# Column sums by adding tiles of every third column, and row moves by transfers, in a two-image attention and DCT kernel

## The reference

```python
yi = jnp.einsum('blc,bqc->blq', wn, xp)              # keys l, queries q
yi = jax.nn.softmax(yi * SOFTMAX_SCALE, axis=1)      # over the keys
yi = yi.reshape(B, L, H, W)
yt = jax.vmap(tconv)(yi, raw_w)                      # 6 x 6 kernel, stride 2
yd = lax.conv_general_dilated(yt, Wd, (2, 2), ((1, 1), (1, 1)), ...)
x = x + (yd + bd) / 6.0
x = x + dct2(groupnorm(x))
```

## Time and profile before

| what | us |
|---|---|
| time, median of 3 runs | 286.29 (285.88 to 287.45) |
| the profiled execution | 286.1 |
| span of its trace | 284.3 |
| PE busy | 216.6 |
| DVE busy | 154.6 |
| ACT busy | 137.5 |
| POOL busy | 94.5 |

### The profile page before, as it was taken

One profiled execution on the slowest core, in us unless ns is written; L12 is line 12 of the kernel. 1 busy time (PEld: TensorE's weight loads), 2 busy tenths in 40 slices (PEclk: granted clock), 3 DMA queues, 4 the chain that ended last, 5 costly groups with the idle time before them and its releaser, 6 DMA issues.

```text
span 284.3 us, 4211 instructions
## 1 busy us (share of the span) xinstructions
PE 216.6 (76%) x1522; PEld 200.9 (71%) x1522; DVE 154.6 (54%) x303; ACT 137.5 (48%) x273; POOL 94.5 (33%) x96
## 2 busy tenths in 40 slices
PE   0064755653647998699998999999898999995085
PEld 0033735553537997699998999999787999994083
DVE  1863134477444367567656554577878544535812
ACT  1366053955866655575776553766454331221030
POOL 8300106063522973149306161596184000000000
PEclk9999999955755999799999999999999999999555
DMA  7206985000200009910000000004000000000502
GB/s 184 35 5 89 101 117 141 1 2 0 42 15 0 3 0 100 113 18 2 2 0 2 0 2 0 2 0 85 1 1 2 0 2 0 2 0 0 109 18 42
DMA packets 9059, 8.82 MB, mean 31 GB/s; under 512 B 7696, under 2 KB 7696, under 8 KB 8560
## 3 DMA queue, kind: packets, MB, share of 16 engines
q1 hardware_dynamic: 9040, 8.56, 18.8%
HBM read 3.32 MB, written 1.18 MB: 16 GB/s over the span
## 4 chain that ended last, share of the span: by engine, by line
PE 48%; DVE 20%; ACT 12%; issue 9%; SPq 5%; DMA 3%; POOL 2%; DVEq 0%; ACTq 0%; POOLq 0%
PE zt L629 22%; PE yt L644 8%; PE ps L609 6%; DVE negm L1010 4%; DVE bnst L893 4%; PE pm L676 3%; DVE yl L1025 3%; ACT nt L807 2%; SPq L363 2%; ACT zneg L749 2%; PE pd L656 2%; ACT z L751 2%; DVE v L1048 2%; DMA v<-mimg 2%; SPq L359 2%
## 5 line engine op out<-in xcount | busy, mean ns | idle before, releaser
L629 PE MATMUL zt<-ident,nt 128*125 128x128 f32 (+1 forms) x720 | 90.6, 277 | 0.0
L629 PEld LDWEIGHTS zt<-ident,nt 128*125 128x125 f32 (+1 forms) x720 | 87.4, 179 | 0.8
L478 POOL TENSOR_TENSOR nt<-nt 128x599 f32<-128x599 f32 (+1 forms) x42 | 56.9, 1354 | 32.2 <-ACT nt L815 25.0
L1025 DVE TENSOR_TENSOR yl<-zt,yh 125x384 fp32r<-125x384 f32 (+1 forms) x60 | 33.4, 557 | 46.2 <-ACT yh L823 18.2
L823 ACT ACTIVATE yh<-zt 125x384 fp32r<-125x384 f32 (+1 forms) x60 | 29.2, 486 | 36.9 <-PE zt L629 36.9
L807 ACT ACTIVATE nt<-ps,negm 128x576 f32<-128x576 f32 x32 | 23.8, 742 | 44.6 <-DVE negm L1010 44.6
L468 POOL TENSOR_TENSOR ml<-vim,mh 128x384 fp32r<-128x384 f32 x12 | 12.3, 1029 | 61.9 <-ACT mh L783 61.8
L815 ACT ACTIVATE nt<-nt,rps 128x599 f32<-128x599 f32 x36 | 28.7, 797 | 5.0 <-DVE rps L1017 4.8
L1048 DVE SCALAR_TENSOR_TENSOR v<-pd,v 32x384 f32<-32x384 f32 (+3 forms) x48 | 26.3, 547 | 2.6 <-PE pd L656 0.9
L1010 DVE TENSOR_REDUCE negm<-ps 128x1 f32<-128x576 f32 x32 | 24.1, 753 | 4.9 <-PE ps L609 4.7
L644 PE MATMUL yt<-yh,kh 125*128 125x384 f32 (+1 forms) x60 | 24.4, 407 | 2.5 <-DVE yl L1025 2.4
(11 more groups left out here) (121 smaller groups left out, 349.3 us busy)
## 6 DMA issues: line engine op xcount, KB each, us to landing
vim<-mimg SPq DMA_DIRECT2D x4, 432.0 KB, 8.2
xn<-x SPq DMA_DIRECT2D x6, 192.0 KB, 3.4
v<-mimg SPq DMA_DIRECT2D x6, 144.0 KB, 6.9
xn<-x SPq DMA_DIRECT2D x6, 96.0 KB, 2.5
v<-x SPq DMA_DIRECT2D x2, 288.0 KB, 4.7
vim<-mimg SPq DMA_DIRECT2D x2, 288.0 KB, 11.9
x_copy<-v SPq DMA_DIRECT2D x2, 288.0 KB, 2.7
xr<-x_copy SPq DMA_DIRECT2D x4, 144.0 KB, 2.9
```

The costliest lines, as they stand in the source:

```text
L478: pool.tensor_tensor(nt[:, dst, (to + 1) * KP + 1:(to + 1) * KP + 1 + n], nt[:, one, (row1 + 1) * KP + 1:(row1 + 1) * KP + 1 + n], nt[:, o ...
L629: last = nc.tensor.matmul(turned(zt[:, m % 2, :], n, dh, col, JW), keys_at(tile, r + dr, n, shift), ident[:, :], start=at == 0, stop=at == ...
L1025: nc.vector.tensor_tensor(yl[0:n, blk, :].rearrange("p (h j) -> p h j", j=W), turned(zt[:, m % 2, :], n), F(yh[0:n, blk, :]).rearrange("p ...
```

## The change

The three tiles of a chunk now hold every third column (tile s the columns s, s + 3, ...). A sum over three neighbouring columns is then a sum of whole tiles with the keys offset, except at the ends of a triple. Of each chunk, POOL adds the first two tiles (`two_columns`, 128 x 600), DVE adds the third (`three_columns`, 128 x 599), and a block takes six transposes: one from the sum of three, two from `two_columns` and a single tile, and three more single ones. The PSUM columns of a transpose are now three apart, where before they were 16 in a row.

The rows that cross between chunks no longer go through PE. `move_row` moves them with SBUF-to-SBUF transfers that shift a tile by 16 partitions (112 partitions x 652 numbers, three for each edge, twelve in all, on SP's queue), and POOL adds them in `row_sums_over_edge` (twelve additions of 128 x 599). So chunks 4 and 5 also take six transposes a block. `yh` and `yl` have 3 buffers for 5, and POOL zeroes four more tiles and two blocks of 32 partitions x 3 tiles at the start.

```diff
-P0, P1, P2, P3, P4, P5, PAIR0, Z1 = (0, 3), 6, 9, 12, 15, 18, (21, 24), 27
-NTILES = 30
+P0, P1, P2, P3, P4, P5, PAIR0, W0, W5 = 0, 3, 6, 9, 12, 15, (18, 21), 24, 27
+TWO, THREE = 30, 32
+NTILES = 34
+YBUF = 3
...
-NTILE_EDGES = 8
+NTILE_EDGES = 10
...
         def by_column_group(chunk):
 
-            return strided(chunk, 0, (JW, ROWS), (JW * ROWS, TPC), (1, JW))
+            return strided(chunk, 0, (JW, ROWS), (1, JW), (JW * ROWS, TPC))
 
         def in_column_groups(src, t):
 
-            return strided(src, W * t, (W * NCH, ROWS), (JW, TPC), (1, JW))
+            return strided(src, W * t, (W * NCH, ROWS), (TPC, JW), (1, TPC))
...
+            def move_row(b, tiles, t, to, src, dst, moved):
+
+                for s in range(TPC):
+                    sp.wait_ge(s_tiles, NTILE_EDGES)
+                    sp.wait_ge(s_pn, TPC * (NCH * b + t) + s + 1)
+                    if b:
+                        sp.wait_ge(s_wrap, 6 * (b - 1) + (3 if t else 0) + s + 1)
+                    sp.dma_start(nt[dst, to + s, :], nt[src, tiles + s, :]).then_inc(moved[s], 16)
...
             pool.memset(strided(nt[:, 0, :], KP, (PT, NTILES), (KP, HL)), 0.0).then_inc(s_tiles, 1)
+            pool.wait_ge(s_tiles, NTILE_EDGES - 2)
+            pool.memset(nt[96:128, W0:W0 + TPC, :], 0.0).then_inc(s_tiles, 1)
+            pool.wait_ge(s_tiles, NTILE_EDGES - 1)
+            pool.memset(nt[0:32, W5:W5 + TPC, :], 0.0).then_inc(s_tiles, 1)
+            pool.wait_ge(s_tiles, NTILE_EDGES)
...
+            def row_sums_over_edge(s):
+
+                b, i, jb = s // NT_IMAGE - 1, s % NT_IMAGE // TPC, s % TPC
+                if b < 0 or i > 1:
+                    return
+                pool.wait_ge((s_up, s_down)[i][jb], 16 * (b + 1))
+                dst, row, moved, row2 = (P4, -1, W0, 1) if i == 0 else (PAIR0[b], 0, W5, -1)
+                n = KP * HL - 1
+                at, at2 = (row + 1) * KP + 1, (row2 + 1) * KP + 1
+                pool.tensor_tensor(nt[:, dst + jb, at:at + n], nt[:, dst + jb, at:at + n],
+                                   nt[:, moved + jb, at2:at2 + n], ALU.add).then_inc(s_wrap, 1)
...
+            def two_columns(k):
+
+                place, row = sums_of(k)
+                for s in range(2):
+                    wait_row_sums(pool, k, s)
+                if k >= 2:
+                    pool.wait_ge(s_zt, KB * (k - 1))
+                    pool.wait_ge(s_three, k - 1)
...
+                row_sums_over_edge(s)
+                if s >= 8 and s % TPC == 2 and (s - 8) // TPC < NG:
+                    two_columns((s - 8) // TPC)
...
                 if blk == 0:
-                    pe.wait_ge(s_add, NSUMS * b + SUMS_FOR[i])
+                    pe.wait_ge(s_two, k + 1)
+                    wait_row_sums(pe, k, 2)
+                    pe.wait_ge(s_three, k + 1)
...
-                sources = ([(Z1, 0, 0)], [(P1, -1, 0)], [(P2, -1, 0)], [(P3, -1, 0)],
-                           [(P4, -1, 0), (P0[b], 1, -1)], [(PAIR0[b], 0, 0), (P5, -1, 1)])[i]
-                work = [(place + jb, dr, dh, JW * jb + dj, -dj) for place, dr, dh in sources
-                        for jb in range(TPC) for dj in (0, -1, 1)]
-                for at, (tile, dr, dh, col, shift) in enumerate(work):
-                    last = nc.tensor.matmul(turned(zt[:, m % 2, :], n, dh, col, JW), keys_at(tile, r + dr, n, shift),
+                work = [(TWO + k % 2, 0, 0, 0), (place + 2, row, -1, 3), (place + 2, row, 0, 2), (place + 1, row, -1, 2),
+                        (place, row, 1, -1), (THREE + k % 2, 0, 0, 1)]
+                for at, (tile, dr, shift, col) in enumerate(work):
+                    last = nc.tensor.matmul(turned(zt[:, m % 2, :], n, col, TPC), keys_at(tile, r + dr, n, shift),
...
+            def three_columns(k):
+
+                place, row = sums_of(k)
+                dve.wait_ge(s_two, k + 1)
+                wait_row_sums(dve, k, 2)
+                if k >= 2:
+                    dve.wait_ge(s_zt, KB * (k - 1))
+                n, at = KP * HL - 1, (row + 1) * KP + 2
+                nc.vector.tensor_tensor(nt[:, THREE + k % 2, KP + 1:KP + 1 + n], nt[:, TWO + k % 2, KP:KP + n],
+                                        nt[:, place + 2, at:at + n], ALU.add).then_inc(s_three, 1)
...
+                if k >= 0 and j == 0:
+                    three_columns(k)
```

More of the change, by code:

```diff
@@ L31 @@
 NT = B * NCH * TPC
+NT_IMAGE = NCH * TPC
 NG = B * NCH
@@ L156, in program @@
         nt = sb("nt", [128, NTILES, PT])
-        yh = sb("yh", [128, KB, CHUNK], F32R)
-        yl = sb("yl", [128, KB, CHUNK], F32R)
+        yh = sb("yh", [128, YBUF, CHUNK], F32R)
+        yl = sb("yl", [128, YBUF, CHUNK], F32R)
         kh = [sb(f"kh{b}", [128, KB, 128], F32R) for b in range(B)]
@@ L254, in program @@
         s_add = sem("row_sums")
+        s_wrap = sem("row_sums_over_tile_edge")
+        s_up = sems("rows_moved_up", TPC)
+        s_down = sems("rows_moved_down", TPC)
+        s_two = sem("two_columns_added")
+        s_three = sem("three_columns_added")
         s_zt = sem("sums_turned")
@@ L326, in by_column_group, with sums_of, wait_row_sums, turned @@
         def by_column_group(chunk):
-            return strided(chunk, 0, (JW, ROWS), (JW * ROWS, TPC), (1, JW))
+            return strided(chunk, 0, (JW, ROWS), (1, JW), (JW * ROWS, TPC))
         def in_column_groups(src, t):
-            return strided(src, W * t, (W * NCH, ROWS), (JW, TPC), (1, JW))
-        def turned(bank, rows, dh=0, col=0, width=W):
-            return strided(bank[0:rows, :], GP * (1 + dh) + 1 + col, (GP, ROWS), (1, width))
+            return strided(src, W * t, (W * NCH, ROWS), (TPC, JW), (1, TPC))
+        def sums_of(k):
+            b, i = k // NCH, k % NCH
+            return ((P0, 0), (P1, -1), (P2, -1), (P3, -1), (P4, -1), (PAIR0[b], 0))[i]
+        def wait_row_sums(eng, k, s):
+            b, i = k // NCH, k % NCH
+            if i < 4:
+                eng.wait_ge(s_add, sums_done(b, ("z1", "z2", "z3", "z4")[i], s))
+            else:
+                eng.wait_ge(s_wrap, 6 * b + 3 * (i - 4) + s + 1)
+        def turned(bank, rows, col=0, every=1):
+            return strided(bank[0:rows, :], 1 + col, (GP, ROWS), (every, W // every))
         @block.sync
@@ L392, in _ @@
                 im2col(b, mimg, s_mimg[b], W, Q, vim, v2, s_mim[b])
+            move_down(0)
+            move_up(1)
             for b in range(B):
+                if b:
+                    move_down(b)
                 sp.wait_ge(s_fin, 4 * NCH * (b + 1))
@@ L643, in values @@
                 for at, (e, y) in enumerate(((kh, yh), (kh, yl), (kl, yh))):
-                    last = nc.tensor.matmul(yt[:, 0:CHUNK], e[b][0:n, blk, :], y[0:n, blk, :],
+                    last = nc.tensor.matmul(yt[:, 0:CHUNK], e[b][0:n, blk, :], y[0:n, (KB * k + blk) % YBUF, :],
                                             start=blk == 0 and at == 0, stop=blk == KB - 1 and at == 2)
```

40 lines of the change are left out of this document (24 added, 16 removed).

## The result

| | before | after |
|---|---|---|
| time, median | 286.34 us (285.88 to 287.45) | 292.70 us (292.38 to 293.17) |
| span of the profiled execution | 284.3 | 291.2 |
| mean granted clock of TensorE | 0.902 | 0.833 |

The ratio is 1.0209, with an interval of 1.0176 to 1.0242: the changed kernel is slower by 6.4 us, where 280.2 was forecast. PE is busy 20 us less, and yet the kernel takes longer. These lines of the page of the changed kernel answer to the earlier trace rows: busy times, the clock in 40 slices, the chain that ended last by engine.

The account below looks back on a forecast made before the run. PE bounds groups 4, 5 and 9 to 11; a DVE/ACT chain hardly touching PE bounds other score groups. Terms 1.7 + 0.3 + 1.6 + 5.6 - 4.7 + 1.2 - 11.6 = -5.9 from 286.1 gave 280.2 us, range 273.5 to 287.5.

Parts of the forecast that it names:

- rival D: PE's clock falls to 1.2 GHz in groups 9 to 11, doubling 23 us of work: +15, 295 us; chance 0.04.
- the ring: Groups with scores: chain from exponential through rps, scaling, yh, yl, negm to the next exponential; 13.0 us in group 2.
- Rival B: Transposes in groups 9 to 11 and 0: scattered PSUM columns cost PE about +6, 286 us; chance 0.12.
- Rival E: PE remains the bound everywhere: 39 us less, 247 us; chance 0.02.
- Start, +1.7: Added memsets on POOL delay the power to about 11.9 us, all of it on the path: +1.7 us.
- Split, +0.3: First split, with neighbouring elements 128 apart, which the first scores wait for: +0.3 us.
- rival C: The split's stride makes ml and mr take 2.0 us each on POOL: slower, 290.2 us; chance 0.12.
- Collision, 8 x 0.8: three_columns on DVE waits while POOL runs ml, in groups k = 0 to 7: 0.8 us a group.
- the prediction's own sign against it: The forecast is wrong if three_columns (L1104) on DVE never exceeds 0.9 us.
- POOL's fullest group: POOL's row sums 8.67, two_columns 1.45 and split 2.0 make 12.1 us, inside the group's 13.0.
- rival A: No collision between three_columns and POOL: 8 x 0.8 less, 273.8 us; chance 0.17.
- Group 9, 10.4: Group without scores, set by DVE's order: 9.3 us, 10.4 with two cosine parts, one hidden in PE's wait.

Follow-up runs that it names:

- warm_pe: The changed kernel with 18 extra identity transposes on PE ahead of turn(k, 0) in groups 1 to 11: 286.44 us, ratio 0.9943.
- six_only: The kernel before with six transposes a block and nothing added, its sums incomplete: 265.91 us, ratio 0.9245.
- no_edge: The changed kernel without the twelve edge additions on POOL, the transfers kept: 296.71 us, ratio 1.0321.
- combo: The changed kernel with pixel-order split, two memsets moved later, only turn(k, 0)'s last transpose waiting, 14 extra transposes from k = 2: 277.57 us, ratio 0.9690.
- whole_split: The changed kernel with mh, ml and mr in pixel order and scores reading every third column as weights: 289.67 us, ratio 1.0044.
- strided_only: The kernel before with only the split's stride added (mh, ml, mr written 128 apart), result columns permuted: 290.75 us, ratio 1.0133.
- combo_few: combo with the 14 extra transposes only in groups 2 to 9: 277.28 us, ratio 0.9636.

## Why the prediction was wrong

**The step that failed**: the sum has no term for the clock. What put it at nothing is a sentence of rival D, "The longest new wait is about 2 us, and only once a group". The same text had PE waiting over 3 us a group in groups with scores, from 13.0 less 9.7, and did not put that number into the rival. Measured were 3.22 and 3.59 us in one piece, and 1.6 to 2.5 in most others. The slow clock followed at the ends of groups 2, 3, 5, 6, 7 and 8 and, from the last, through most of group 9; in groups 10 and 11, where D had it too, it did not come. A PEclk of 0.5 after 125 us was the prediction's own sign of being wrong, and it stands there from 143 us on. Its price by warm_pe is 9.8 us in groups 2 to 11 at least, of the 10.8 (134.32 - 123.5) by which these groups missed the forecast. With the clock held these groups come to 124.5 for the forecast's 123.5, but part of that is luck: groups 3, 4 and 5, and 7 took 2.8 us less than forecast, group 9 took 2.9 more. That the measured 292.7 is near rival D's 295 is luck as well: D had the loss in groups 9 to 11, and they took 34.2 for the forecast's 28.4. By D's own numbers, 23 us of work doubled and no waits, it would have been 46 - 28.4 = 17.6 and not 15.

**What was right.** That a faster PE gives groups 2 and 3 some 0.3 us: six_only has 0.4 in each. The size of the ring: group 2 at 13.0 (13.23 with the clock held), groups 4 and 5 at 26.2 (26.6, and 25.2 with the clock held), groups 10 and 11 at 10.0 and 8.0 (10.12 and 8.04). PE waits for L1104. The edge additions lay in slack (no_edge). The edge transfers and `YBUF` show in no wait looked at here, but no run takes them out. Rival B is out: six transposes take 0.66 us on the chain, 0.11 each, as before, so columns three apart cost PE nothing (on combo's chain, `zt L710 x6`). Rival E is out.

**Start, +1.7**: the power came at 11.42, 1.17 later, where 11.9 was expected. Taking the two memsets out brought it to 9.69 and `tl` of k = 1 forward by 2.35. The power of undelayed kernels stands between 9.69 and 10.25, so the size was about right.

**Split, +0.3, and rival C.** The term was mis-sized, and on the wrong engine. The prediction asked what POOL's additions would cost; ACT's two copies had not been priced, and they cost 0.36 and 0.38 us more in each group. The first scores came 2.14 later (48.25 for 46.11), 1.17 with the power and 0.97 behind it; whole_split takes 0.73 of that back. With what it moved under POOL's row sums, strided_only puts it at 4.3 us before group 2. That is enough for the 2.0 by which the part up to k = 1 was missed (5.6 for 3.6), though the parts do not add up (below). Rival C's own condition, 2.0 us for `ml`, did not come about on its own; 1.78 did, beside `three_columns`. The Trainium skill (SBUF — State Buffer, Specifications) wants two hits in a 16-byte line; ACT's 0.51 to 0.88 agrees in direction, and so does the slower loading of weights that lie 12 bytes apart. POOL's addition, 1.0 to 1.2, feels little of it.

**Collision, 8 x 0.8.** It came the other way round: `three_columns` took 0.77 or 0.78 eleven times of twelve (1.05 at 245.59), nearly the prediction's own sign against it, and `ml` took up to 1.78. It is not that ACT's slower copy made `ml` late: in combo the copy is short again, the two start within 0.05 us of each other, and DVE takes 0.77 to 0.79 there too while `ml` takes 1.6. The size of the ring came out nonetheless in group 2, by another way, since POOL, with no pause, held `three_columns` up by 1.49 us: the 12.1 us estimated for POOL's fullest group were 13.1 (133.21 to 146.32), and no slack was left. By the forecast's own working rival A should have come out there; POOL's lateness took the collision's place. In groups 3, 4 and 5, and 7 the 0.8 is missing, as A has it.

**Group 9, 10.4**: with the clock held it takes 13.28, of which 2.12 are extra transposes on the chain, and 11.35 in combo_few. The term was 0.9 short. The layout had put one of two cosine parts into PE's wait, and had left out a third piece. On the chain of combo_few all three stand:

```profile
224.12 0.58 PE pm L747 x16
...
227.79 1.48 PE pm L757 x16
...
231.18 1.49 PE pm L757 x16
```

The rest of 16.03, some 4.7, is put down to the clock, which was at the lower level from 231.4 to 241.7 and is at 1.00 there in combo_few.

**What stays open**: what, besides the length of a wait, lets the clock fall (1.63 us did and did not, in one kernel), and how the 5.6 us before group 2 divide between stride, memsets and the clock of the first groups; the parts measured alone, 4.3 and 2.35, come to more than the whole, and the power's own 0.5 us of scatter is among them.

## What to carry to other kernels

Before taking work off an engine that is the bound, write down its longest idle stretch in every stage afterwards, and price all of its work behind that stretch at the slow clock as well: here 20 us of gain were paid back with 27, some 10 of them in clock. Write down, too, what a new operation on the chain makes the others wait: DVE's twelve additions of 0.78 us went with 12 us. Let the last instruction that needs an operand wait for it, not the first of its group: one moved wait was worth 8 us. When a layout changes, price each access that writes or reads it on every engine, and where the layout makes one engine write with a stride, see whether another with time to spare can read with it.
